# A two-layer recurrent block on one core: the scan's work shared anew over VectorE, GpSimd and ScalarE, routing and LayerNorms cut into smaller pieces

## The reference

```
def _combine(left, right, W):                       # 4 lanes of 32 channels
    v = ((left + right) @ W)
    att = softmax(einsum('btld,btmd->btlm', left, right) * 32 ** -0.5)
    z = rms_norm(einsum('btlm,btmd->btld', att, v)) / (1 + lane)
    return left + z
d = 1
while d < T:                                        # T = 512: nine levels
    x = _combine(concat([identity] * d, x[:, :-d]), x, W)
    d *= 2
```

## Time and profile before

| | |
|---|---|
| median of 3 runs | 639.1 us (638.64 to 639.62) |
| profiled execution | 638.24 us |
| its span, first to last instruction | 636.5 us |
| mean granted TensorE clock | 0.945 of full speed |
| busy: TensorE, VectorE, GpSimd, ScalarE | 532.1, 525.6, 397.3, 261.9 us |

### The profile page before, as it was taken

How to read it: one execution, slowest core, us unless ns; L and a number is a source line. 1 busy time by engine, 2 the same in 40 slices (tenths; PEclk the granted TensorE clock), 3 DMA queues, 4 the chain that set the end, 5 groups by cost and what they waited for, 6 DMA issues and landing times.

```text
span 636.5 us, 8860 instructions
## 1 busy us (share of the span) xinstructions
PE 532.1 (84%) x2918; PEld 410.6 (65%) x2918; DVE 525.6 (83%) x993; ACT 261.9 (41%) x607; POOL 397.3 (62%) x367
## 2 busy tenths in 40 slices
PE   4979999999999992759888888888888888886855
PEld 3746666665666661748676776776776776775635
DVE  7576857856865664498999999999999999999875
ACT  3332332252252242035446446445455455454232
POOL 6920011032032059537999999999999999999954
PEclk9999999999999996597999999999999999999676
DMA  8330000000000000100111111101101111101002
GB/s 249 119 132 2 1 1 1 1 2 16 0 2 17 1 0 17 34 0 18 34 33 34 35 33 33 50 18 51 34 18 50 34 33 34 34 18 33 18 1 66
DMA packets 16598, 20.79 MB, mean 33 GB/s; under 512 B 2344, under 2 KB 10160, under 8 KB 16428
## 3 DMA queue, kind: packets, MB, share of 16 engines
q1 hardware_dynamic: 16556, 20.26, 10.5%
HBM read 9.76 MB, written 1.05 MB: 17 GB/s over the span
## 4 chain that ended last, share of the span: by engine, by line
DVE 40%; PE 31%; issue 17%; ACT 5%; POOL 5%; DMA 0%; DVEq 0%; ACTq 0%; POOLq 0%
PE bank L569 30%; DVE shared L1437 9%; DVE bank L1449 9%; DVE shared L1443 7%; ACT shared L1094 3%; DVE shared L1472 2%; PE bank L572 2%; POOL wgu_lo L462 1%; DVE shared L1457 1%; DVE ssum L1467 1%; ACT shared L1092 1%; DVE shared L1302 1%; DVE smax L1453 1%; DVE shared L1307 1%; POOL wgu_hi L460 1%
## 5 line engine op out<-in xcount | busy, mean ns | idle before, releaser
L569 PE MATMUL bank<-xnT_lo,wgu_hi 128*128 128x512 f32 x264 | 121.1, 459 | 8.7 <-ACT shared L1106 6.9
L569 PE MATMUL bank<-w,shared 128*128 128x128 f32 x1024 | 121.1, 277 | 0.0
L569 PEld LDWEIGHTS bank<-w,shared 128*128 128x128 f32 x1024 | 118.4, 194 | 0.2 <-ACT shared L1106 0.2
L569 PE MATMUL bank<-xnT_hi,wgu_lo 128*128 128x512 f32 x264 | 105.7, 400 | 0.0
L569 PE MATMUL bank<-xnT_hi,wgu_hi 128*128 128x512 f32 x264 | 105.3, 399 | 0.0
L512 POOL TENSOR_TENSOR shared<-shared 128x1024 f32<-128x1024 f32 x36 | 85.1, 2365 | 27.3 <-DVE shared L1472 27.3
L569 PE MATMUL bank<-shared 128*128 128x512 f32 (+3 forms) x280 | 89.4, 440 | 1.9 <-ACT shared L953 1.2
L1449 DVE TENSOR_REDUCE bank<-shared 128x64 f32<-128x2048 f32 x36 | 82.6, 2295 | 3.9 <-POOL shared L494 2.7
L1106 ACT ACTIVATE shared<-bank,b_now 128x512 f32<-128x512 f32 x128 | 80.6, 682 | 0.3
L975 ACT ACTIVATE shared<-bank 128x512 f32<-128x512 f32 x68 | 40.6, 598 | 94.1 <-PE bank L569 91.0
L1302 DVE TENSOR_TENSOR shared<-shared,bank 128x512 f32<-128x512 f32 x64 | 43.8, 685 | 40.5 <-PE bank L569 30.1
(11 more groups left out here) (180 smaller groups left out, 880.7 us busy)
## 6 DMA issues: line engine op xcount, KB each, us to landing
w<-in_w SPq DMA_DIRECT2D x8, 256.0 KB, 3.1
shared<-in_w SPq DMA_DIRECT2D x1, 2048.0 KB, 9.2
left_tok<-state_ext SPq DMA_DIRECT2D x16, 128.0 KB
left_tok<-state_ext SPq DMA_DIRECT2D x8, 192.0 KB
shared<-in_wd SPq DMA_DIRECT2D x1, 1088.0 KB, 11.7
x<-in_x SPq DMA_DIRECT2D x4, 256.0 KB, 3.9
out<-x SPq DMA_DIRECT2D x4, 256.0 KB, 2.3
left_tok<-state_ext SPq DMA_DIRECT2D x4, 254.0 KB
```

Source lines behind the costliest of these rows:

```text
L569: return nc.tensor.matmul(out, lhsT, rhs, start=start, stop=stop)
```

## The change

In the scan:
- VectorE multiplies all four lanes in `products` of odd batches, and in `mix_values` always; GpSimd's `last_product` is left for even batches, its `last_mix` and ScalarE's `values_out` go.
- `add_lanes` moves from VectorE to GpSimd, behind `halve_mix`.
- ScalarE multiplies the down product by the gates, tile by tile in bank 7 (`gated`; for expert 0 into `acc`, which needs no clearing then), and VectorE adds the whole bank to `acc` in one instruction, for experts 1 to 7.
- `square_sum` moves on VectorE from before `exp_sum` to behind `mix_values`.
- Biases and gates are read in place; the copies `b1_now` and `gate1_now` go. VectorE's loop over levels is written out.

In layer 0:
- The routing of the next batch is cut in eight pieces, at p = 1, 3, 5, 8, 9, 12, 13, 14; its gates are transposed and copied at p = 15.
- The LayerNorms are cut in statistics and moments, in neighbouring units (p = 6, 7 and 10, 11).
- GpSimd's `split_expert` 0 to 7 stand between its other work of the last batch, and only a diagonal of `ecmp` is cleared.

The core of the diff (functions that are only cut in two or dropped are shortened):

```
@@ gpsimd: order of batch 3, then the scan's slot @@
-            for b in range(B):
+            for b in range(B - 1):
                 state_product(b)
                 ...
                 attention_tokens(b)
+            state_product(B - 1)
+            token_rest1(B - 3)
+            pool.wait_ge(s("ld_w1"), 16)
+            split_expert(0)
+            add_to_x(B - 2)
+            for e in range(1, 6):
+                split_expert(e)
+            normalise1(B - 2)
+            attention_tokens(B - 1)
+            split_expert(6)
             token_rest1(B - 2)
-            pool.wait_ge(s("ld_w1"), 16)
-            pool.wait_ge(s("u_mm"), item((B - 1) * PAIRS) + 1)
-            for e in range(E1):
-                split_expert(e)
+            split_expert(7)
             pool.wait_ge(s("x1_done"), B)
-            g.memset(ecmp[:], 0.0).then_inc(s("ecmp_zero"), 1)
-            g.memset(acc[:], 0.0).then_inc(s("acc_zero"), 1)
+            g.memset(ecmp[:].rearrange("p t a b -> p t (a b)")[:, :, 0:E1 * E1:E1 + 1], 0.0).then_inc(s("ecmp_zero"), 1)
 ...
-            def last_mix(k, b):
-                ...
             def halve_mix(k, b):
                 pool.wait_ge(s("mix_done"), k + 1)
-                pool.wait_ge(s("last_mix"), k + 1)
                 ...
+            def add_lanes(k, b):
+                pool.wait_ge(s("mix2_done"), k + 1)
+                m = mix2[:, b % 2].rearrange("p j l m d -> p (j l) m d")
+                g.tensor_tensor(z[:, b % 2].rearrange("p j (l d) -> p (j l) d", l=LANES), m[:, :, 0], m[:, :, 1],
+                                ALU.add).then_inc(s("z_done"), 1)
             def slot(k, b, this=True, before=True, before2=True, ahead=True):
                 if before:
                     halve_mix(k - 1, (b - 1) % B)
+                    add_lanes(k - 1, (b - 1) % B)
                 ...
                 if ahead:
                     sum_inputs(k + 1, (b + 1) % B)
-                    last_product(k + 1, (b + 1) % B)
-                if this:
-                    last_mix(k, b)
+                    if b % 2 == 1:
+                        last_product(k + 1, (b + 1) % B)
@@ tensor @@
-                elif p == 13 and b < B - 1:
-                    gates_to_rows(b + 1)
                 ...
+                if p == 15 and b < B - 1:
+                    gates_to_rows(b + 1)
 ...
             def values(k, b):
                 pe.wait_ge(s("sumT_cp"), k + 1)
-                after(pe, s("v_cp"), k)
                 after(pe, s("mix_done"), k)
 ...
             def expert_down(e, blk, tiles):
-                    after(pe, s("ffn_acc"), n * TB)
+                    after(pe, s("ffn_gated"), n * TB)
+                    after(pe, s("ffn_acc"), n - B)
@@ scalar (gates_out0(b + 1) moves from p == 13 to p == 15) @@
-            def values_out(k, b):
-                ...
             def relu(e, blk, c):
-                a.activation(hT[:, c], bank[UP[c]][:], ACT.Relu, bias=b1_now[:, c:c + 1]).then_inc(s("ffn_relu"), 1)
+                a.activation(hT[:, c], bank[UP[c]][:], ACT.Relu, bias=b1[:, e, c:c + 1]).then_inc(s("ffn_relu"), 1)
+            def gated(e, blk):
+                n = e * B + blk
+                act.wait_ge(s("gate1_done"), 1)
+                act.wait_ge(s("ffn_down"), n + 1)
+                for j in range(TB):
+                    t, y = blk * TB + j, bank[7][:, j * P:(j + 1) * P]
+                    a.activation(acc[:, t] if e == 0 else y, y, ACT.Copy, scale=gate1[:, t, e:e + 1]).then_inc(s("ffn_gated"), 1)
+            def slot(k, b, this=True, before=True, ahead=True, up=None, down=None, then=None):
-                if this:
-                    values_out(k, b)
                 if ahead:
                     left_out(k + 1, (b + 1) % B)
                 ...
+                if down:
+                    gated(*down)
                 if up:
-                    if up[1] == 0:
-                        a.copy(b1_now[:], ...)
-                        act.wait_ge(s("b1_now_done"), up[0] + 1)
                     relu(*up, 0)
                     relu(*up, 1)
                 ...
-                        a.copy(gate1_now[:], ...)
@@ vector: layer 0; route_tops, route_ranks, route_gates, route_parts are cut out of the four old pieces @@
-                elif p == 3 and b < B - 1:
-                    route_groups(b + 1)
-                elif p == 7 and b < B - 1:
-                    route_masks(b + 1)
-                elif p == 9 and b < B - 1:
-                    route_best(b + 1)
-                elif p == 10 and b < B - 1:
-                    route_weights(b + 1)
                 elif p == 6 and b > 0:
                     dve.wait_ge(s("x1_done"), b)
-                    layer_norm(b - 1, "l1_stat", "l1_var")
+                    layer_norm_stats(b - 1, "l1_stat")
+                elif p == 7 and b > 0:
+                    layer_norm_moments(b - 1, "l1_stat", "l1_var")
+                elif p == 10:
+                    attention_stats(b)
                 elif p == 11:
-                    attention_stats(b)
+                    attention_moments(b)
+                if b < B - 1:
+                    if p == 1:
+                        route_groups(b + 1)
                ...
+                    elif p == 14:
+                        route_parts(b + 1)
@@ vector: scan @@
             def products(k, b):
+                lanes = LANES - 1 if b % 2 == 0 else LANES
                 ...
+                tt(prod[:, b % 2, :, :, 0:lanes], left.broadcast_to([P, TB, LANES, lanes, LD]),
+                   right.broadcast_to([P, TB, LANES, lanes, LD]), ALU.mult).then_inc(s("prod_done"), 1)
-            def add_lanes(k, b):
-                ...
             def mix_values(k, b):
-                dve.wait_ge(s("v_cp"), k + 1)
+                dve.wait_ge(s("v_mm"), k + 1)
+                dve.wait_ge(s("sexp_done"), k + 1)
+                ...
-            def expert_sum(e, blk, tiles):
-                dve.wait_ge(s("ffn_down"), e * B + blk + 1)
-                for j in tiles:
-                    t = blk * TB + j
-                    stt(acc[:, t], bank[7][:, j * P:(j + 1) * P], gate1_now[:, t:t + 1], acc[:, t],
-                        ALU.mult, ALU.add).then_inc(s("ffn_acc"), 1)
+            def expert_sum(e, blk):
+                n = e * B + blk
+                if e > 0:
+                    dve.wait_ge(s("ffn_gated"), TB * (n + 1))
+                    part = acc[:, blk * TB:(blk + 1) * TB].rearrange("p j c -> p (j c)")
+                    tt(part, part, bank[7][:], ALU.add).then_inc(s("ffn_acc"), 1)
             def slot(k, b, this=True, before=True, summed=None):
                 prev = (k - 1, (b - 1) % B)
                 if this:
                     products(k, b)
                     scores(k, b)
-                if before:
-                    add_lanes(*prev)
-                ...
                     score_max(k, b)
-                    expert_sum(*summed, range(0, 1))
                     softmax_shift(k, b)
                 if summed:
-                    expert_sum(*summed, range(1, TB))
-                if before:
-                    square_sum(*prev)
+                    expert_sum(*summed)
                 if this:
                     exp_sum(k, b)
                     mix_values(k, b)
+                if before:
+                    square_sum(*prev)
-            with dve.Fori(0, LEVELS - 1) as lev:
+            for lev in range(LEVELS - 1):
```

More of the change, by code:

```diff
@@ L1035, in extras @@
                     attention_roots(b)
-                elif p == 13 and b < B - 1:
-                    gates_out0(b + 1)
                 elif p == 14 and b > 0:
@@ L1041, in extras @@
                     scan_input_out(b - 1, MISC)
+                if p == 15 and b < B - 1:
+                    gates_out0(b + 1)
             def gates_out0(b):
@@ L1080, in left_out @@
                 a.copy(bank[1][:], left_tok[:, b].rearrange("p j c -> p (j c)")).then_inc(s("left_tok_cp"), 1)
-            def values_out(k, b):
-                act.wait_ge(s("v_mm"), k + 1)
-                a.copy(v_last[:, b % 2], bank[2][:].rearrange("p (j c) -> p j c", j=TB)[:, :, (LANES - 1) * LD:]).then_inc(s("v_cp"), 1)
             def expo(k, b):
@@ L1105, in relu @@
                 after(act, s("ffn_down"), e * B + blk)
-                a.activation(hT[:, c], bank[UP[c]][:], ACT.Relu, bias=b1_now[:, c:c + 1]).then_inc(s("ffn_relu"), 1)
-            def slot(k, b, this=True, before=True, ahead=True, up=None, then=None):
-                if this:
-                    values_out(k, b)
+                a.activation(hT[:, c], bank[UP[c]][:], ACT.Relu, bias=b1[:, e, c:c + 1]).then_inc(s("ffn_relu"), 1)
[7 more added lines that the diff above has]
+            def slot(k, b, this=True, before=True, ahead=True, up=None, down=None, then=None):
                 if ahead:
@@ L1132, in slot @@
                     relu(*up, 3)
-                    if up[1] == 0:
-                        act.wait_ge(s("gate1_done"), 1)
```

(16 more changed lines are left out.)

80 lines of the change are left out of this document (37 added, 43 removed).

## The result

| | before | after |
|---|---|---|
| median of 4 runs, us | 639.36 (638.64 to 639.98) | 695.83 (693.77 to 697.38) |
| ratio to before | 1 | 1.0882 [1.0845, 1.0919] |
| span of the profiled execution, us | 636.5 | 692.0 |
| TensorE's granted clock over the span | 0.945 | 0.89 |

A forecast was written before the change was run, and what follows sets the result against it. It took TensorE to bound layer 0 and VectorE the scan, with a longer loop closing after the change. Terms -1.8 - 8.8 + 29.4 - 1.8 = +17.0 on 638.24 us gave 656 us; forecast 646 to 663, 8 in 10 640 to 675.

The forecast's parts named there:

- The loop: Scan slots 6 to 32: a closed chain through the engines' queues makes a slot 10.7 us, +1.09 each, +29.4 us.
- The clock: Scan: TensorE's gap of 2.5 us ahead of `values` in each slot leaves its clock at 2.4 GHz, no cost.
- The clock falls: Rival, scan: TensorE's gap lowers its clock; 675 us if in a third of the slots, 713 in all; 14%.
- Layer 0: Layer 0, bound by TensorE: shorter routing bursts win some of TensorE's waits, net -1.8 us, bounds 0 and -3.
- Hand-over: Between layer 0 and the scan: first scan transposes 7.15 us earlier; mix of slot 0 8.2 us earlier.
- Slots 1 to 5: Early scan slots: expert 0 needs no add, slot 3 takes 9.8 us; 46.2 us against 48.6, -2.4.
- the last slots: Scan slots 33 to 35, without a down product: -1.8 us in all.
- VectorE alone: Scan slot: VectorE's own instructions plus 0.35 us of waiting for exp would give 8.35 us, against 9.62.
- The rival's 597 us: Rival, scan: VectorE sets the slot at about 8.5 us, -30 us over 27 slots, about 597 us; 10% in full form.

The follow-up runs named there:

- e2: The changed kernel with VectorE's expert add moved to the end of its slot, behind the squares' sum; 594.7 us, 0.9291 of before.
- e7: The changed kernel with the gating back on VectorE, four multiply-adds from bank 7 in place of ScalarE's four and the add; 645.39 us.
- e3: The changed kernel with only the squares' sum moved back ahead of row sums and mix, behind the expert add; 643.63 us.
- e1: The changed kernel with 18 extra TensorE products a slot, results unread, in the gap behind the last up product; 656.01 us.
- e4: The kernel before with only the squares' sum moved behind mix; 639.82 us, 1.0011 of before.
- e9: The changed kernel with 5 extra TensorE products (0.75 us) in the gap behind the last up product, results unread; 672.07 us.
- e6: The kernel before with only the routing in eight parts, its gates two units later, and the LayerNorms in two; 633.73 us.

## Why the prediction was right or wrong

**The loop: right.** From the end of one mix (436.88) to the next, forecast and measured: down product starts at M + 2.83 and 2.81, ends at 6.57 and 6.65, add starts at 7.73 and 7.94, mix ends at 10.74 and 10.96 (other slots 10.90). The down product is 3.84 where the earlier trace rows have 3.74, the gating 1.17 plus a wake-up of 0.09. VectorE's wait was forecast at 2.3 and is 2.8. Over 27 slots the term is +34.7 for +29.4. A part of this 5.3 is in the prediction's own arithmetic: its steps give 10.74, but 10.70 went into the sum (1.1 us over 27 slots), and its upper bound of 10.95, which holds, is 0.1 more than its steps give with 1.2 us of gating. The link that decides is the add ahead of mix: with it out of mix's way (e2) a slot is 8.75. The others are worth less: without ScalarE's gating (e7) a slot is 10.13, with the squares' sum back (e3) 10.34, now by another path.

**The clock: the step that failed.** The prediction wrote "My gap is shorter than both, so I forecast 2.4 GHz", from a single gap of 3.24 us that cost nothing. That reading was right: in the trace before, the granted clock is 1.00 from 269.4 to 286.4 us, all around that gap, and 0.51 in the 6.9 us from the end of the gap of 3.70. The gap of the change came out at 2.7 us, and 22 of 27 slots paid: +38.8 us, 1.8 in each on average. e1 shows it, as filling the gap takes 39.8 us away. It does not show that the rest of the sum was exact: by the stages the other terms were off by -3.3 (up to mix of slot 0), -1.8 (slots 0 to 5), +5.3 (the loop) and -0.5 (the end), which by luck cancel to -0.3. The rival "The clock falls" had the mechanism at 14%, and took 2.1 us in a third of the slots, or in all, for 675 or 713; 696 lies between. The gap's length gave no bound: one row of a gap that stands by itself doesn't answer for the same gap in every slot. The kernels together show it (the gap ahead of `values`, for e3 also the one ahead of the transposes):

| kernel | gap in each slot, us | slots with a long down product |
|---|---|---|
| e1 | 0.53 | none |
| e4 | 1.48 | none |
| e3 | 1.5, and 1.0 or 0.4 | none |
| e7 | 1.9 | 3 of 28 |
| e9 | 2.1 | 9 of 27 |
| after | 2.7 | 22 of 27 |

The Trainium skill (TensorE: Matmul & The Clock Gate, What's actually happening) ties the low clock to recent idleness. The kernels with one gap agree, from 1.5 us (none) to 2.7 us (22 of 27 slots); e3 adds that the same idle time in two gaps cost nothing. The rival that the page stood beside deserved the larger chance.

**Layer 0: right in kind, and outside its bounds, -5.0 for -1.8.** The forecast took the waits of TensorE for L1307, 2.2 us, and 0.8 for the polar step, as all that could be won, and put the lower bound at -3. In the profile after, the same view for 44 to 230 us has

```profile
PE bank L569 <- DVE shared L1328: 1.1, 2, 0.9
```

where L1328 is L1307 by its new line, so these waits gave only 1.1. The busy time of the same stretch, before and after, with the same 769 instructions of TensorE in it:

```profile
44.00:235.00 191.00, 185.83 (x769) 120.36 (x770) 135.92 (x408) 63.14 (x112) 29.93 (x45) 1.00 0.01 4
...
44.00:230.00 186.00, 184.16 (x769) 120.97 (x770) 136.41 (x408) 62.81 (x112) 41.37 (x57) 1.00 0.01 4
```

TensorE's idle time fell by 3.3 us, from 5.2 to 1.8, which is already more than the bound: the forecast counted two rows of the waits and left out the smaller ones. The other 1.7 us came off the busy time: records of matmuls seem to hold part of a stall, so idle time alone understates what can be gained (the runs don't show in which records). e6 measures the term by itself, -5.1 by the medians. In its own profiled execution, the longest of its four, mix of slot 0 starts only 2.2 earlier, as the clock there is 0.83 from 36 to 56 us.

**Hand-over: right.** The first transposes of slot 0 start at 245.74 for 257.90: 12.16 earlier, 5.0 of it layer 0's and 7.16 the hand-over's, for 7.15. The normalisations are at 0.34 as forecast, x's add at 0.69:

```profile
L1194 DVE TENSOR_SCALAR xn<-x,ln_mv,ln_rstd x4: 341/342/346, 239.6 to 240.3; 128x128 f32<-128x128 f32 x4
```

Mix of slot 0 is 8.3 earlier without layer 0, for 8.2.

**Slots 1 to 5 and the last slots: right in kind.** From the first products of slot 1 to the end of mix of slot 5 it is 44.7 us for 48.6 before, -3.8 for -2.4: slot 3 takes 8.4 us and not 9.8. The end gives -1.8 for -1.3, both counted between starts of mix.

**VectorE alone: 0.4 short.** Its sum was forecast at 8.35 us, or 8.5 with GpSimd; e2, where VectorE sets the slot, has 8.46 and 8.99, a mean of 8.75. Most of the difference is in three steps. Score reduce and maximum are 2.33 and 0.26 us start to start, priced at 2.20 and 0.13, and products of four lanes 2.32, priced at 2.20: in the new order each of them is followed at once by the instruction that reads its result, which before held only for the products. The rival's 597 us and e2's 594.7 agree by luck: e2's 27 slots gained 23.5 and not the rival's 30, and the stages ahead of them gained more than forecast. What separates this rival from the kernel after is the place of one call.

## What to carry to other kernels

When work is shared anew among engines that each run their queue in order, don't add up each engine's work: follow one slot's cycle through all the queues, from an instruction back to its own next instance. The consumer of a long chain on another engine (here the expert add, which mix doesn't read) belongs at the end of the slot; ahead of mix it closed a loop that, with the clock that fell in it, cost 101 us. And a gap of TensorE that recurs in each slot is priced with the clock: here nothing up to 1.5 us, most of the slots at 2.7, so that filling it with products nobody reads gained 39.8 us. When the total of a forecast agrees with a run, compare its terms too: here four of them were off and cancelled.

## What the hardware showed beyond that

- The clock fell after gaps of 1.9 to 2.7 us, shorter than the one of 3.24 us that had cost nothing, and for part of a product too: the down product (32 matmuls) took 3.84, 4.21, 4.49, 5.47 or 5.77 us, by slot and kernel.
- The same idle time cost nothing when it was split: e3 idles 1.5 and then 1.0 or 0.4 us in each slot at a clock of 1.00, e9 only 2.1 us in one piece, and 9 of 27 slots pay.
- An instruction of VectorE that reads what its direct predecessor wrote starts some 0.13 us later: from the score reduce to the maximum it is 2.33 us (e2), where with another instruction between it was 2.20.
- A change in GpSimd's phase alone turned VectorE's add of the lanes from 1.75 us to 1.13 (e4).
